# Attention scores in two halves of TensorE's array, with q and k as two fp32r parts in place of three bf16 ones

## The chip, the cores and the metric

The kernel runs on one core of one Trainium2 chip. The metric is the device time of one execution in microseconds; the span is the time from the first to the last instruction of the program in the profile. Engines are named as in the profile: PE (TensorE), DVE (VectorE), ACT (ScalarE), POOL (GpSimd), SP (SyncE, whose queue issues most DMAs).

## The reference

Four sequences of 1024 tokens with 256 features pass a linear attention block and a transformer block with a mixture of experts:

```
x = x + attn(layernorm(x))            # (x Wtheta)(x Wphi)^T (x Wg) / 16
h = rmsnorm(layernorm(x)); q, k, v = h @ wqkv     # 16 heads of 16, 4 kv heads
q, k = rope(q), rope(k)
probs = softmax(causal(q k^T / 4)); x2 = ln(x) + (probs v) @ wo
h = rmsnorm(x2); top 2 of 8 experts, weights normalised
out += (silu(h w1[e]) * (h w3[e])) @ w2[e] * weight       # FFN 512
```

The expert choice is sensitive to small errors, so scores are formed with nearly full fp32 precision.

## The kernel before

**Batches and groups.** The work is cut into four batches (one sequence each). A batch is projected (xn, gram, theta, x1, h, v, k_mm, q1_mm, q2_mm), then its four kv heads are taken one after the other as groups of four query heads (`GRP`), 16 groups in all. A group has two chunks `r` of 512 queries; a chunk has key tiles `kt` of 128 keys.

**Split and stack.** After rope (DVE), q and k are split: the sum (stage `split`, i = 0), a bf16 part (ACT), the rest (POOL), a second bf16 part (ACT), a third. In batch 0 the first and last step are on DVE, later on POOL. They go to DRAM (`qk_parts`) and come back as a stack of 96 rows: pairs of parts (`KPARTS` = 3, 2, 1, so that the products hi x hi, hi x mid, ... stand in the rows of one contraction), once for the keys and once for each of the four heads. Two more rows hold the negated row maximum. There are three stacks, for the group at work and the ones ahead.

**Maxima.** Ahead of a chunk's scores PE forms all scores in the other orientation (stage `max`, L2137 to L2145). DVE takes the maximum of each row (L1932 for the second chunk with a custom instruction that adds the mask, L1934 for the first, where PE adds the mask as a bf16 matmul of an identity). PE transposes the maxima (`maxT`), DVE negates and splits them, SP writes them into the stack.

**Scores.** For each key tile PE forms the scores of the heads (L2157, one matmul a head, one PSUM bank for up to 512 columns), ACT takes the exponential (L1440), POOL masks the diagonal tile (L1292), and PE multiplies with v (`pv`, L2171: four heads in four column tiles of the array, side by side). x1 (L2090) is the one stage that works in two 64-row tiles.

**Experts.** Routed rows are scattered to DRAM (POOL), fetched in 71 blocks of 128 rows, and a block is one round of `blockT` (L2191), `up` (L2209 to L2213), `gatedT` (L2219) and `down` (L2231 to L2237). The first blocks use fp32 weights, later ones fp32r weights in two parts. The expert's offset is read from `bexp` by PE right ahead of a block's first `up` matmul.

**Order.** A planner, `plan()`, which runs when the kernel is built, writes out one order of steps for each engine from costs (`work_of`), due times (streams with `spread_over`) and hand-set shifts of them (`NUDGE`). Each engine follows its list in order and waits on semaphores. PSUM has seven banks in a ring. Where the plan would leave PE idle it puts short filler matmuls (`warm`, L2046). The third buffer of probabilities lies over the experts' `gated` buffer, which therefore waits for batch 2.

## Time and profile before

| | |
|---|---|
| median of 3 runs | 1060.29 us (1058.63 to 1061.31) |
| the profiled execution: time | 1058.78 us |
| the profiled execution: span | 1057.1 us |
| busy: PE, DVE, ACT, POOL | 1011.6, 789.2, 661.5, 435.5 us |

A PE row of the profile has the form of the array as rows*columns: 98*128 is 98 rows of contraction and 128 columns of weights, 64*128 a matmul in one of two halves of the rows, 128*17 one of four column tiles. fp32 matmuls are profiled as two records, transposes and fp32r ones as one.

### The profile page before, as it was taken

Reading aid. Unit: us, or ns where it says so; the run is one execution under the profiler, and the core shown is the slowest. Engines: PE = TensorE matmul, PEld = TensorE weight load, DVE = VectorE, ACT = ScalarE, POOL = GpSimd, SP = SyncE. Lnnn points to the kernel's source line nnn. Section 1 sums busy time; section 2 is a strip of 40 time slices with the busy share of each in tenths; the row PEclk is TensorE's granted clock in tenths of the full one; section 3 lists DMA queues with packets and bytes.
Section 4 is the critical chain, followed back from the end, with each engine's and each line's share of the span. In section 5 each row is a group of like instructions: output and inputs, shape, how many; then the busy total and the mean of one; then the engine's idle time right before and its main releaser. Section 6 shows DMA issues by size and latency. Waiting matters only on the chain.

```text
span 1057.1 us, 19430 instructions
## 1 busy us (share of the span) xinstructions
PE 1011.6 (96%) x6264; PEld 594.6 (56%) x6264; DVE 789.2 (75%) x1701; ACT 661.5 (63%) x1305; POOL 435.5 (41%) x476
## 2 busy tenths in 40 slices
PE   5999999999999999999999999999989999999997
PEld 4765335443453333453334444456678888888886
DVE  5689979787778998899857997136776666666664
ACT  3562785747768878847767656684534555555553
POOL 1020145155732144422545325457477543444443
PEclk9999999999999999999999999999999999999999
DMA  6433114132336557732343412243434333222220
GB/s 200 128 123 103 53 46 143 55 115 77 97 109 194 146 188 212 203 95 82 111 120 109 137 25 70 52 92 82 103 78 98 73 57 52 48 47 46 48 46 11
DMA packets 86642, 102.33 MB, mean 97 GB/s; under 512 B 17904, under 2 KB 74224, under 8 KB 86544
## 3 DMA queue, kind: packets, MB, share of 16 engines
q1 hardware_dynamic: 72240, 81.46, 26.3%
q0 software_dynamic: 14304, 19.63, 10.1%
q8 instruction: 53, 0.87, 0.4%
q14 instruction: 45, 0.37, 0.1%
HBM read 56.22 MB, written 41.01 MB: 92 GB/s over the span
## 4 chain that ended last, share of the span: by engine, by line
PE 74%; DVE 16%; ACT 5%; issue 3%; DMA 1%; POOL 1%; DVEq 0%; ACTq 0%; POOLq 0%
PE psum L2171 10%; PE psum L2157 9%; PE psum L2209 6%; PE psum L2213 5%; PE psum L2137 5%; PE psum L2210 5%; DVE psum L1932 5%; PE psum L2211 5%; PE psum L2123 3%; PE psum L2219 3%; PE psum L2237 3%; PE psum L2140 2%; PE psum L2231 2%; PE psum L2233 2%; PE psum L2232 2%
## 5 line engine op out<-in xcount | busy, mean ns | idle before, releaser
L1440 ACT ACTIVATE probs_mem<-psum 128x512 f32<-128x512 f32 (+1 forms) x464 | 232.0, 584 | 90.2 <-PE psum L2157 89.0
L1932 DVE CUSTOM_DVE_ANT_1 psum<-psum,masking 128x640 f32<-128x640 f32 (+3 forms) x256 | 257.2, 1045 | 32.9 <-PE psum L2140 32.1
L1337 POOL DMA_INDIRECT out<-yout,labels x71 | 133.7, 1884 | 182.9 <-DMA out<-yout,labels 86.8
L2157 PE MATMUL psum<-stack_mem 98*128 98x512 bf16 (+3 forms) x768 | 169.3, 327 | 3.3 <-DVE mx L1932 1.8
L1292 POOL TENSOR_SCALAR_AFFINE_SELECT probs_mem<-probs_mem 128x512 f32<-128x512 f32 x104 | 66.9, 644 | 223.9 <-ACT probs_mem L1440 223.6
L2157 PEld LDWEIGHTS psum<-stack_mem 98*128 98x128 bf16 x768 | 64.6, 97 | 105.3 <-issue 21.9
L2171 PE MATMUL psum<-probs_mem,v 128*17 128x512 f32 (+3 forms) x1152 | 117.1, 490 | 0.8 <-POOL probs_mem L1292 0.5
L2015 DVE TENSOR_TENSOR w_lo<-w_mem,w_hi 128x1024 fp32r<-128x1024 f32 x51 | 62.5, 1225 | 65.5 <-PE psum L2233 57.3
L1934 DVE TENSOR_REDUCE mx<-psum 128x4 f32<-128x512 f32 (+2 forms) x96 | 96.1, 1036 | 13.1 <-PE psum L2145 10.8
L2137 PE MATMUL psum<-stack_mem 96*128 96x512 bf16 x256 | 95.2, 383 | 5.4 <-DVE mx L1932 2.6
L2209 PE MATMUL psum<-w_hi,x_hi 128*128 x216 | 93.6, 433 | 6.2 <-issue 2.4
L1440 ACT ACTIVATE gated<-psum 128x512 f32<-128x512 f32 x144 | 79.2, 612 | 24.9 <-PE psum L2157 24.9
L2210 PE MATMUL psum<-w_lo,x_hi 128*128 x216 | 85.9, 398 | 0.0
L2211 PE MATMUL psum<-w_hi,x_lo 128*128 x216 | 85.7, 397 | 0.0
L2028 DVE SCALAR_TENSOR_TENSOR gated<-gated,psum 128x512 f32<-128x512 f32 x71 | 48.3, 680 | 46.2 <-ACT gated L1465 45.9
L1458 ACT ACTIVATE yout<-psum,labels 128x256 f32<-128x256 f32 x71 | 33.8, 476 | 73.6 <-PE psum L2233 45.1
L1322 POOL DMA_INDIRECT routed<-hrow,route_mem x64 | 67.7, 1057 | 24.3 <-issue 13.4
L2140 PE MATMUL psum<-stack_mem 96*128 96x128 bf16 (+3 forms) x256 | 76.3, 298 | 0.0
L2137 PEld LDWEIGHTS psum<-stack_mem 96*128 96x128 bf16 x256 | 24.8, 97 | 76.4 <-DVE mx L1932 34.8
L2213 PE MATMUL psum<-w_mem,blockT 128*128 x136 | 65.1, 598 | 1.0 <-issue 1.0
L2231 PE MATMUL psum<-w_hi,g_hi 128*128 128x256 f32 x204 | 61.6, 302 | 0.9 <-DVE g_lo L2006 0.9
L2032 DVE TENSOR_TENSOR gated<-psum,gated 128x512 f32<-128x512 f32 x71 | 49.0, 691 | 17.9 <-PE psum L2213 11.7
(229 smaller groups left out, 2070.8 us busy)
## 6 DMA issues: line engine op xcount, KB each, us to landing
block<-routed SPq DMA_DIRECT2D x71, 129.0 KB, 2.5
w_mem<-in_w13T SPq DMA_DIRECT2D x16, 512.0 KB, 4.9
qk_parts<-w_mem SPq DMA_DIRECT2D x16, 384.0 KB, 2.9
stack_mem<-qk_parts SPq DMA_DIRECT2D x32, 192.0 KB, 3.3
w_mem<-in_x SPq DMA_DIRECT2D x8, 512.0 KB, 5.1
out<-w_mem SPq DMA_DIRECT2D x8, 512.0 KB, 4.0
x_late<-out SPq DMA_DIRECT2D x8, 512.0 KB, 5.0
stack_mem<-qk_parts SPq DMA_DIRECT2D x32, 128.0 KB, 2.7
```

What stands on the lines that cost most here:

```text
L1337: e.indirect_dma_start(out_rows, bass.IndirectOffsetOnAxis(ap=labels[w % NLABEL].bitcast(I32)[:, 0:1], axis=0), youts[w % NYOUT], None, bo ...
L1440: e.activation(probs[probs_of(m)][:, hh:hh + n, q0:CH], grid(turn[step][0][:, 0:n * (CH - q0)], n), ACT.Exp, scale=float(HD) ** -0.5).then ...
L1932: e.tensor_tensor_reduce(keys, keys, masked(w), 1.0, -3e38, ALU.add, ALU.max, to).then_inc(sem["max"], 1)
L1934: e.tensor_reduce(to, took, AX.X, ALU.max).then_inc(sem["max"], 1)
L2137: e.matmul(bk[:, 0:CH], rows_of, s[0:STACK, 0, GRP, :], start=True, stop=True)
L2140: m = e.matmul(to, rows_of, s[0:STACK, r, GRP, 0:w], start=True, stop=True)
L2157: m = e.matmul(bk[:, i * (CH - q0):(i + 1) * (CH - q0)], s[0:STACK + NMAX, kt // TPR, GRP, kt % TPR * P:(kt % TPR + 1) * P], s[0:STACK + N ...
L2171: m = e.matmul(pv_bank[32 * hh:32 * hh + HD + 1, q0:CH], v1[:, b, kt, g, :], pb[:, hh, q0:CH], start=(kt == KEYS[r][0]), stop=(kt == KEYS[ ...
L2209: e.matmul(bk, x_hi[w % 2][:, k], w13_hi[k][:, of], start=first, stop=False)
L2210: e.matmul(bk, x_hi[w % 2][:, k], w13_lo[:, k, of], start=False, stop=False)
L2211: m = e.matmul(bk, x_lo[w % 2][:, k], w13_hi[k][:, of], start=False, stop=final)
L2213: m = e.matmul(bk, blockT[w % 2][:, k], w13_s[:, k, of], start=first, stop=final)
```

## The change

- q and k are split into two fp32r parts (`KPARTS` = 2, 1): 48 rows. The rounding is by ACT, the rest is the last step; the POOL step and one ACT step of the split are gone. `qk_parts` and the stacks are fp32.
- A stack holds the keys twice, in rows 0 to 49 and in rows 64 to 113, and two heads beside each, so that heads 0 and 1 lie in the one half of the array and heads 2 and 3 in the other. `HEAD_ORDER` takes heads 0, 2, 1, 3. A load is four DMAs in place of two. fp32r matmuls are at least 256 columns wide (`formed`). Score steps cover at most two heads, where a tile of 128 columns took four.
- Two parts of a block (`youts`, `blockT`, one of `blocks`) lie over the third stack, so batch 3 has two stacks (`stack_of`), and the blocks that use them wait for batch 2's last group.
- Of norm1 and norm2 of batches 1 to 3, and of all norm3, DVE does the first steps and the seed; the Newton steps and what follows are on POOL (13 to 18 instructions in a chain). The seed is one instruction in place of two.
- PE reads the next block's offset in the middle of the second half of `up`.
- The planner has new costs for max and score (half of the columns), and new `NUDGE` values.

```diff
-KPARTS = (3, 2, 1)
+KPARTS = (2, 1)
+HALF_ROWS, NSLOTS = P // 2, GRP // 2
+HEAD_ORDER = [s + h * NSLOTS for s in range(NSLOTS) for h in range(2)]
...
-TURN, LIKE = 0.1, (3.1, 0.06)
+TURN, LIKE = 0.1, (6.9, 0.03)
...
+        columns, formed = CH + w if r else nh * w, CH + max(w, 2 * P) if r else nh * max(w, 2 * P)
+        return ("PE", formed / 4800 + 0.02 if r else formed / 4800 + nh * P / 2400 + 0.12), ...
...
-            return ("PE", n * w / 2400 + 0.01), ("ACT", 0.06 + n * w / 1200)
+            return ("PE", n * w / 4800 + 0.02), ("ACT", 0.06 + n * w / 1200)
...
 NUDGE = {
-        "aggr": {(0,): -126.5},
+        "aggr": {(3,): -18.1},
...
+                    for half in range(2):
+                        r0, heads = half * HALF_ROWS + to, slice(half * NSLOTS * CH, (half + 1) * NSLOTS * CH)
+                        e.dma_start(s[r0:r0 + nk * HD, c, NSLOTS, :], ...)
+                        e.dma_start(s[r0:r0 + nk * HD, c, 0:NSLOTS, :]..., ...)
...
+                    if r:
+                        rows = tile_rows(h0, STACK)
+                        rows_of = s[rows, r, h0 % NSLOTS, jj * P:(jj + 1) * P]
+                        e.matmul(bk[:, 0:CH], rows_of, s[rows, 0, NSLOTS, :], start=True, stop=True)
+                        m = e.matmul(bk[:, CH:CH + formed], rows_of, s[rows, r, NSLOTS, 0:formed], start=True, stop=True)
+                    else:
+                        in_bank = CH // pitch
+                        for slot_of in range(in_bank):
+                            for i in range(2):
+                                ...
+                                e.matmul(to, s[rows, r, at_slot, jj * P:(jj + 1) * P], s[rows, r, NSLOTS, 0:formed], start=slot_of == 0, stop=False)
+                        for i in range(2):
+                            own = grid(bk[:, i * CH:(i + 1) * CH], in_bank)[:, :, w - P:w]
+                            m = e.matmul(own, identb, causal.unsqueeze(1).broadcast_to([P, in_bank, P]), start=False, stop=True)
...
+                    rows, first = tile_rows(hh, STACK + NMAX), hh % NSLOTS
+                    e.matmul(grid(bk[:, 0:n * (CH - q0)], n), s[rows, kt // TPR, NSLOTS, kt % TPR * P:(kt % TPR + 1) * P],
+                             s[rows, r, first:first + n, q0:CH], start=True, stop=True).then_inc(sem["score_mm"], 1)
...
+                        if half == 1 and first and (gi, c + 1) in WORK:
+                            offset[w + 1] = e.value_load(bexp[gi][0:1, c + 1:c + 2], min_val=0, max_val=(NE - 1) * 2 * FFN)
```

How the order of instructions moves. On PE, the first chunk's maxima of a group before: L2150 is `maxT`, L2133 and L2145 the bf16 masks, L2142 and L2144 the maxima, L2171 is `pv`.

```order
L2150 MATMUL psum<-ident,mx 16x128
L2133 MATMUL psum<-masking,identb 128x512
L2142 MATMUL psum<-stack_mem 128x128 x4
L2144 MATMUL psum<-stack_mem 128x256
L2145 MATMUL psum<-masking,identb 128x128
L2144 MATMUL psum<-stack_mem 128x256
L2145 MATMUL psum<-masking,identb 128x128
```

After, at the same place (L2306 is `maxT`, L2298 the maxima in halves, L2301 the masks over the whole array, L2200 a filler):

```order
L2200 MATMUL psum<-ident 128x128
L2306 MATMUL psum<-ident,mx 16x128
L2298 MATMUL psum<-stack_mem 128x256 x4
L2301 MATMUL psum<-masking,identb 128x2x128 x2
L2298 MATMUL psum<-stack_mem 128x256 x4
L2301 MATMUL psum<-masking,identb 128x2x128 x2
L2298 MATMUL psum<-stack_mem 128x384 x2
L2301 MATMUL psum<-masking,identb 128x128 x2
```

All of the upper rows but L2150 are full-array matmuls; of the lower ones L2298 is in halves and L2301 is not, so the form changes at every row.

The second chunk's maxima among scores on PE, before (L2137 and L2140 are one unit of maxima, L2157 scores, L2171 `pv`):

```order
L2157 MATMUL psum<-stack_mem 128x128 x4
L2137 MATMUL psum<-stack_mem 128x512
L2140 MATMUL psum<-stack_mem 128x128
L2171 MATMUL psum<-gated,v 17x256 x4
L2137 MATMUL psum<-stack_mem 128x512
L2140 MATMUL psum<-stack_mem 128x128
L2157 MATMUL psum<-stack_mem 128x512 x4
```

And after (L2290 and L2291 the unit, L2313 scores, L2326 `pv`):

```order
L2313 MATMUL psum<-stack_mem 128x384
L2290 MATMUL psum<-stack_mem 128x512
L2291 MATMUL psum<-stack_mem 128x256
L2326 MATMUL psum<-gated,v 17x512 x4
L2313 MATMUL psum<-stack_mem 128x384 x3
L2290 MATMUL psum<-stack_mem 128x512
L2291 MATMUL psum<-stack_mem 128x256
L2313 MATMUL psum<-stack_mem 128x512
L2326 MATMUL psum<-probs_mem,v 17x512 x4
```

The mix is as before, but the two matmuls of a unit lie in one half, and a run in halves ends at each `pv`.

In the expert blocks on PE, before (L2219 is `gatedT`, L2209 and L2210 the first `up` matmuls):

```order
L2219 MATMUL psum<-ident,gated 128x128 x4
L2200 TENSOR_LOAD bexp
L2200 ISA x2
L2209 ISA
L2209 MATMUL psum<-w_hi_49,x_hi_58 128x512
```

And after, in the second half of a block's `up` (L2364 to L2366 are its matmuls):

```order
L2366 MATMUL psum<-w_hi_51,x_lo_61 128x512
L2370 TENSOR_LOAD bexp
L2370 ISA x2
L2364 REGISTER_ALU
L2364 MATMUL psum<-w_hi_52,x_hi_59 128x512
```

The read moved from behind the transposes to a place among the matmuls of the block before.

## Rows read from the trace of the kernel before

**Rows 1.** The page's first part: busy us, share, instructions.
```profile
PE 1011.6 (96%) x6264; PEld 594.6 (56%) x6264; DVE 789.2 (75%) x1701; ACT 661.5 (63%) x1305; POOL 435.5 (41%) x476
```
**Rows 2.** Busy time by stretch, then granted clock, DMA share, GB/s.
```profile
0.00:73.00 73.00, 60.63 (x337) 44.57 (x338) 48.76 (x192) 40.02 (x82) 12.11 (x24) 1.00 0.46 140
73.00:131.00 58.00, 56.13 (x371) 27.32 (x369) 56.71 (x129) 28.57 (x57) 5.05 (x8) 1.00 0.33 99
131.00:537.00 406.00, 392.94 (x2693) 171.17 (x2689) 343.00 (x763) 293.83 (x605) 166.47 (x194) 1.00 0.42 125
537.00:685.00 148.00, 145.14 (x931) 64.33 (x926) 99.72 (x236) 98.10 (x211) 65.76 (x81) 1.00 0.30 83
685.00:800.00 115.00, 108.66 (x487) 77.72 (x486) 68.83 (x143) 59.62 (x114) 70.54 (x65) 0.99 0.40 89
800.00:1057.00 257.00, 248.08 (x1461) 209.50 (x1459) 172.17 (x241) 141.37 (x241) 115.56 (x105) 1.00 0.30 51
```
**Rows 3.** Timeline of PE from 340 us: start, duration, then the instruction.
```profile
340.50 0.38 PE L2140 MATMUL psum<-stack_mem 96*128 96x512 bf16 x1
340.72 0.38 PE L2137 MATMUL psum<-stack_mem 96*128 96x512 bf16 x1
```
**Rows 4.** Timeline of PE from 902 us, in an expert block.
```profile
902.43 0.28 PE L2233 MATMUL psum<-w_hi,g_lo 128*128 128x256 f32 x1
902.55 0.60 PE L2219 MATMUL psum<-ident,gated 128*128 128x128 f32 x4
903.13 0.50 PE L2209 MATMUL psum<-w_hi,x_hi 128*128 x1
903.46 0.39 PE L2210 MATMUL psum<-w_lo,x_hi 128*128 x1
903.69 0.40 PE L2211 MATMUL psum<-w_hi,x_lo 128*128 x1
```
**Rows 5.** Timeline of PE from 171 us: scores, x1 in halves, a projection.
```profile
170.81 0.60 PE L2157 MATMUL psum<-stack_mem 98*128 98x512 bf16 x2
171.34 0.70 PE L2090 MATMUL psum<-w_mem 64*128 64x256 f32 x4
171.97 1.55 PE L2123 MATMUL psum<-w_mem 128*128 128x512 f32 x3
```
**Rows 6.** Timeline of the weight loads at the same place.
```profile
172.50 0.19 PEld L2123 LDWEIGHTS psum<-w_mem 128*128 128x128 f32 x1 [0.24 <-issue]
172.93 0.19 PEld L2123 LDWEIGHTS psum<-w_mem 128*128 128x128 f32 x1 [0.24 <-issue]
```
**Rows 7.** Timeline of PE from 28 us: x1's steps of batch 0.
```profile
28.04 2.19 PE L2090 MATMUL psum<-w_mem 64*128 64x256 f32 x16
30.15 0.38 PE L2046 MATMUL psum<-ident 128*128 128x128 f32 x1
```
**Rows 8.** Groups of DVE by form: busy, mean ns of one, idle before.
```profile
L1536 DVE SCALAR_TENSOR_TENSOR scales<-rt,scales 128x16 f32<-128x16 f32 x9 | 2.5, 279 | 0.3
L1536 DVE SCALAR_TENSOR_TENSOR rstd<-rt,rstd 128x8 f32<-128x8 f32 x12 | 2.0, 165 | 0.4
```
**Rows 9.** Groups of POOL by form.
```profile
L1302 POOL TENSOR_TENSOR x_late<-x_late,hrow 128x256 f32<-128x256 f32 x32 | 23.6, 757 | 29.6 <-DVE hrow L1956 29.4
L1297 POOL COPY hrow<-ids_s 128x8 int32<-128x8 int32 x3 | 1.2, 413 | 0.0
```
**Rows 10.** Groups of POOL and ACT by form: two steps of the split.
```profile
L1283 POOL TENSOR_TENSOR w_mem<-w_mem 128x512 f32<-128x512 f32 x16 | 18.4, 1163 | 15.2 <-ACT w_mem L1430 15.2
L1433 ACT ACTIVATE w_mem<-w_mem 128x512 bf16<-128x512 f32 x16 | 10.2, 638 | 2.4 <-POOL w_mem L1283 2.4
```
**Rows 11.** One line's instructions: SP's issue of a stack load, ns min/median/max.
```profile
L1141 SPq DMA_DIRECT2D stack_mem<-qk_parts x96: 429/580/1818, 62.6 to 571.7; - x96
```
**Rows 12.** Waits of the weight loads of the scores: us in total, times, longest.
```profile
PEld psum L2157 <- issue: 21.9, 48, 0.9
PEld psum L2157 <- ACT probs_mem L1440: 17.8, 44, 0.9
```

More of the change, by code:

```diff
@@ L99, with stack_of, stack_freed @@
 HEAD_GROUPS = [(b, g) for b in range(NBATCH) for g in range(NKV)]
+LAST_TRIPLE = (NBATCH - 1) * NKV
+assert LAST_TRIPLE % NSTACK == 0
+def stack_of(n):
+    if n < LAST_TRIPLE:
+        return n % NSTACK, n // NSTACK
+    return (n - LAST_TRIPLE) % 2, LAST_TRIPLE // NSTACK + (n - LAST_TRIPLE) // 2
+def stack_freed(n):
+    at, use = stack_of(n)
+    return [m for m in range(n) if stack_of(m) == (at, use - 1)]
+LAST_IN_TAIL = HEAD_GROUPS[LAST_TRIPLE - 1]
 def max_units(r):
     if r:
-        return [(jj, hh, 1, CH, (jj + 1) * P) for jj in range(TPR) for hh in range(GRP)]
+        return [(jj, hh, 1, CH, (jj + 1) * P) for jj in range(TPR) for hh in HEAD_ORDER]
     units = []
@@ L108, in max_units, with heads_of @@
         w = (jj + 1) * P
-        nh = GRP if jj < 2 else 2
-        units += [(jj, h0, nh, w if jj < 2 else CH, w) for h0 in range(0, GRP, nh)]
-    return units
+        units += [(jj, 0, GRP, CH // NSLOTS, w)] if w <= CH // NSLOTS else [(jj, s, 2, CH, w) for s in range(NSLOTS)]
+    return units
+def heads_of(unit):
+    jj, h0, nh = unit[:3]
+    return slice(h0, None if nh == 2 else h0 + nh, NSLOTS if nh == 2 else 1)
 def max_banks(r, u):
-    return 1 if not r and max_units(r)[u][0] == 0 else 2
+    return 2
 def banks_of(step):
@@ new lines @@
+        "rank": {(0,): -34.3},
+        "recip": {(1,): -57.6},
+        "recip_store": {(3,): -37.2},
+        "route": {(0,): -24.3, (1,): -32.9, (2,): 12.1},
+        "score": {(0, 0, 0): -19.1, (0, 1, 0): 0.4, (0, 2, 0): -130.5, (0, 3, 0): 13.3, (0, 3, 1): -1.8, (1, 0, 1): 3.2, (1, 1, 0): 1.5, (1, 1, 1): 0.1, (1, 2, 1):
+        -1.5, (2, 1, 1): 31.4, (2, 2, 1): -68.5, (2, 3, 0): -7.1, (3, 0, 1): -70.9, (3, 1, 0): -26.3, (3, 1, 1): -149.9, (3, 3, 0): -57},
+        "split": {(1,): -7.1},
+        "spread": {(1,): 23.1},
@@ L288 @@
+        "square": {(3,): -81.4},
+        "stack": {(0, 1, 0): -70.9, (2, 1, 0): 7.9, (2, 2, 0): 43.6, (2, 3, 0): -54.3},
+        "stats": {(3,): 31.9},
+        "stats2": {(0,): 30.2, (1,): 12.1},
+        "v": {(2,): -34.5},
+        "w2": {(): 3},
+        "weight": {(0,): 4.2},
+        "wo": {(2,): -39.1},
+        "x1": {(1,): 10.4, (2,): -5.7},
+        "xhat": {(2,): -20},
+        "xnT": {(2,): 18},
 }
@@ L538, in project @@
                 continue
-            steps += [(half, ("norm1", b, i)) for i in one_part(b, half, NORM1_STEPS)] + [(half, ("xn", b, j)) for j in (range(TPB) if b else tiles)]
+            steps += [(half, ("norm1", b, i)) for i in one_part(b, half, norm_steps("norm1", b))] + [(half, ("xn", b, j)) for j in (range(TPB) if b else tiles)]
         steps += [(2, ("gram", b, i)) for i in range(gram_steps(b))] + [(2, ("square", b, i)) for i in range(2)]
@@ L817, in over, with late @@
             return nc.alloc_sbuf_tensor_at(name, shape, F32R, offset=at)[:]
+        def late(name, n, at):
+            return nc.alloc_sbuf_tensor_at(name, [P, n], F32, offset=at)[:]
         def carve(mem, sizes):
@@ L1022, in buffer_loaded, with tile_rows @@
         def buffer_loaded(q, b, g, r):
-            n = b * NKV + g
+            at, use = stack_of(b * NKV + g)
             for c in range(r + 1):
-                q.wait_ge(f"stack{n % NSTACK}_{c}", 16 * 2 * len(KPARTS) * (n // NSTACK + 1))
+                q.wait_ge(f"stack{at}_{c}", 16 * 4 * len(KPARTS) * (use + 1))
+        def tile_rows(head, n):
+            first = head // NSLOTS * HALF_ROWS
+            return slice(first, first + n)
         def stack_read(q, b, g):
@@ L1269, in _, with norm3_rest, go_on @@
+            def norm3_rest(b):
+                q.wait_ge("norm3", NORM3_SEED * (b + 1))
+                t = rt[:, 2]
+                yield from newton("norm3_rest", rstd2, t[:, 1], t[:, 2], t[:, 3])
+            def go_on(make, b):
+                if (make, b) not in chains:
+                    chains[make, b] = make(b)
+                next(chains[make, b])
             for step in orders["POOL"]:
                 stage, *at = step
-                if stage == "split":
+                if stage == "norm1":
+                    go_on(norm1_rest, at[0])
+                elif stage == "norm2":
+                    go_on(norm2_rest, at[0])
+                elif stage == "norm3":
+                    go_on(norm3_rest, at[0])
+                elif stage == "split":
@@ L1587, in norm3 @@
                 yield
-                yield from rsqrt("norm3", rstd2, t[:, 1], t[:, 2], t[:, 3])
+                seed("norm3", rstd2, t[:, 1])
+                yield
             def route(gi):
@@ L2196, in _ @@
                     q.wait_ge("blockT_out", w + 1)
-                    if half == 0:
+                    if half == 0 and w not in offset:
                         q.wait_ge("route", routed(gi, "all"))
```

319 lines of the change are left out of this document (181 added, 138 removed), and 4 rows, old and new, of the table WORK_OF.

## The prediction

> **What bounds the kernel now.** I read the page's first two parts, then the table of stretches, then TensorE's timeline in four short windows, matmul by matmul. TensorE is busy in 96% of the span, VectorE in 75% [rows 1], at a granted clock of 1.00 in all stretches but one (0.99) [rows 2]. The table has six stretches: projection of batch 0 (to 73 us), the first maxima (to 131), attention of batches 0 to 2 (131 to 537), of batch 3 with some expert blocks (537 to 685), and expert blocks alone (685 to 1057). In 73 to 131 VectorE is the limit: 56.71 us busy of 58. In 131 to 537 both are full, TensorE 392.94 and VectorE 343.00 of 406. From 685 on VectorE has a third of its time free and TensorE has not [rows 2].
>
> "Busy" of TensorE counts a matmul's latency, so I priced it by the distance from one start to the next. A bf16 matmul of 512 columns takes 0.22 us (340.50, 340.72) [rows 3]; over many of them it is 0.216, and narrower ones are in proportion. An fp32r matmul of 512 columns takes 0.23 (903.46 to 903.69), one of 256 columns 0.12 (902.43 to 902.55); of four transposes' 0.60, some 0.16 is the last one's latency beyond its slot (as 0.28 over 0.12 in the row ahead), so they take 0.44, each 0.11 [rows 4]. Two more prices matter here. First, a change of the tile form: two bf16 matmuls and then four 64*128 ones start at 170.81 and 171.34, 0.53 us for what is 0.43 otherwise, so leaving a form costs about 0.09 [rows 5]; I use 0.092, the same between all forms here. Second, the first weights after a change are not loaded ahead: the L2123 matmul that starts at 171.97 is followed by the next load at 172.50, 0.53 later, and that by one at 172.93, 0.43 later, so 128 fp32 columns of weights cost 0.10 more once [rows 5, 6].
>
> Walking the order of TensorE's 6264 profiled matmuls with these prices gives 961 us of array time; the span is 1057. Of 131 to 537 it fills 380 of 406: 26 us are waits.
>
> **The scores and maxima.** Before, they are 294,912 columns of scores and 327,680 of maxima with their masks, 622,592 in all, by 0.216/512 us: 263 us. After, scores have as many columns, the maxima 311,296 of fp32r (narrow ones are formed 256 wide) and 32,768 of bf16 masks: 606,208 x 0.233/512 = 276 us one at a time, and 14 us of masks. The operands now have 48 or 50 rows and lie in one half of the array, so that two can run side by side. That this happens at all is in the trace: x1's 16 records of two 64-row halves take 2.11 us from 28.04 to 30.15, with 0.3 of it a wait; a pass over 512 fp32 columns takes 0.43, so one over 256 takes 0.21, and 16 in a row would need 3.4 [rows 6, 7]. But in-order issue pairs only what stands next to each other. A unit of the second chunk's maxima is two matmuls in the same half (L2290, L2291); it overlaps only with a neighbour's. Walking the changed order, matmul by matmul, 90 us of the 276 are overlapped, not 138. Term: 276 - 90 + 14 - 263 = **-63 us**.
>
> **The changes of form.** The order has 401 changes of tile form before and 735 after: score and P.V changed form already (full and column tiles), but now every bf16 mask, every transposition, projection or filler between two scores or maxima is a change too; there are 330 separate runs in halves, 96 of them of two matmuls only. 334 more changes x 0.092 = **+30 us**. Each run in halves starts with fp32r weights that nothing loaded ahead (both halves' loads go together, as x1's do): 320 such entries x 0.105 = 34, and with other fp32 entries **+39 us**. Together with five more fillers the walk gives 966 us of array time after, against 961: **+5 us**. So the doubled array gives back nearly all that it wins.
>
> The Trainium skill's "TensorEngine Tiling (Array Packing)", Overview, gives up to 2x for a contraction of 64 or less, and under Tiling Modes says that changing the mode drains TensorE. The first by itself would make the scores and maxima 152 us in place of 200, and the sum 48 lower; the second is what rows 5 price, and it speaks against this change.
>
> **The experts' offset.** Before, PE reads a block's expert right ahead of its first matmul. After the four transposes of 902.55 the next matmul comes at 903.13 where 0.44 would do, 0.14 late, and its successor 0.33 after it in place of 0.23: 0.24 us a block [rows 4]. In blocks that still use fp32 weights in one piece the read is covered. The read moves behind three matmuls of the half before, where TensorE's queue has some microseconds of work ahead: 50 blocks x 0.245 = **-12 us**. If that cover is gone, the term is 0.
>
> **VectorE and the norms.** 116 VectorE instructions go (1189 to 1073), the norm chains of batches 1 to 3 and all of norm3, at 0.17 to 0.28 us [rows 8]: 23 us off VectorE. They count only where it is the limit: 36 of them in 60 to 131, 7 us, of which I take 5 for the first maxima. In 131 to 537 about 16 us of VectorE go, under TensorE's 380: of the 26 us of waits I take 5. GpSimd gets 151 small instructions in chains of 13 to 18. No such one is in the trace: the nearest rows are a copy of 8 columns at 0.413 us and a two-operand one of 256 at 0.757 [rows 9]; from below, 0.17 as on VectorE. I take 0.35, near the first row since the width is 8 or 16: a chain takes about 6 us where VectorE's took 2.8. It stands in GpSimd's queue among masks, and ScalarE's xn, h or h2 stands behind it, and exponentials behind those. The projections are spread over a whole group's scores, so I take it as hidden; uncovered, ten chains cost up to 32 us.
>
> **The split** loses a GpSimd step of 1.163 and a ScalarE one of 0.638 [rows 10]; 24 of each are off the limit, once, before the first stack is loaded, they lie on the path. Of the 1.8 I take **-1**, since VectorE is behind at that time. ScalarE gets 32 more exponentials (four heads of 128 columns were one): 32 x 0.2 = 6 us against 15 removed, no term.
>
> **The stacks.** SP issues 64 more DMAs (659 to 723) at 0.580 us [rows 11]: 16 for a group in place of 12. Until batch 3 they are a group ahead. In batch 3 there are two stacks, so a group's load waits for the group two before: 16 x 0.58 + 3 = 12 us from there to its last maxima, while the next group's scores and expert blocks (5.8 us each) are there for TensorE. I take 0; if PE's fixed order meets a late stack, 3 to 5 us for each of two groups. The late buffers over the third stack wait for batch 2, as the blocks did for the third set of probabilities: nothing.
>
> **The sum:** +5 - 12 - 5 - 5 - 1 = -18 us. The profiled execution took 1058.78 us at a span of 1057.1; the three runs have a median of 1060.29, 1.5 above it. So 1060.3 - 18 = **1042 us**.
>
> **The rivals.**
> - *Two halves at full speed* (0.14). Waits on banks hold a score back until its neighbour is there, or the order's short runs cost less than x1's. By the page's 2x the sum is 48 lower: 994; with the weights' exposure hidden in half of the runs, 20 lower, 1022. For it: x1's loads do go in pairs. Against: every entry in rows 5 and 7 pays, and 190 of 330 runs are of two to four matmuls. I put 990 to 1022 here.
> - *No change* (0.11): the halves do what I say, and the norms on GpSimd hold ScalarE up on seven of ten chains by 2.6 us each: 1042 + 18 = 1060.
> - *Slower: the halves do not meet* (0.23). Without any overlap the order's array time is 1063, 97 more than 966, and the time 1139. A full-array matmul hid a sequencer that came 0.2 us late; a half that waits 0.2 us for its neighbour's bank runs alone. From 18 us of 90 on, one overlap in five lost, the change is slower than before; with a third lost, 1042 + 30 = 1072. For it: 21.9 us of the loads of L2157 waited for "issue" alone, and 17.8 for ScalarE [rows 12]. Against: TensorE now comes later than its plan, so banks are free when it arrives.
> - *The change does not do what it says*: a half-array matmul takes the whole array's time, that is the 1139 above (0.02 of the 0.23), since x1 shows otherwise.
> - *The forecast* (0.52): 1023 to 1057.
>
> **The range.** 0.14 lies at or below 1022, 0.23 above 1063. I leave out some 0.08 at each end: **1014 to 1082**. Around 1060.3, 0.3% is 3 us, about what such a measurement can tell: faster 0.52 + 0.14 = 0.66, same 0.11, slower 0.23.
>
> **What will show it.** In the changed trace: consecutive scores of two halves start under 0.02 us apart, the next pair 0.23 later; the first pair of a run takes 0.33; about 735 changes of form; time of scores and maxima near 200 us plus 70 for changes. The block in the last stretch takes 4.87 us, not 5.12. VectorE is busy about 766 us. If the first group's end (131 us) is not 5 us earlier, the VectorE term is wrong; if 131 to 537 grows, overlap is lost; if ScalarE waits for GpSimd in xn or h, the chains are not hidden. The forecast is wrong if the waits of 131 to 537 do not stay near 25 us.

## The result and the profile after

The changed kernel took 1106.7, 1109.7, 1128.3 and 1128.3 us, median 1119.0, against 1059.6 for the kernel before on the same chip. The ratio is 1.046, 95% interval 1.042 to 1.049, made without the two executions of 1128, in which the granted clock was 0.93 in place of 0.95. Its fastest execution is 47 us slower than the kernel before; 1042 was forecast and 1082 was the upper end of the range.

The profiled execution (1109.7 us, span 1108.0) has, in the page's first two parts, PE's busy share and, over 40 slices of the span, the clock that TensorE was granted in tenths:

```profile
PE 1055.0 (95%) x6130; PEld 636.1 (57%) x6130; DVE 773.0 (70%) x1585; ACT 654.7 (59%) x1313; POOL 429.7 (39%) x603
```

```profile
PEclk9998999799999989896889999799999999999999
```

PE is as busy as before [rows 1]. But the clock row has dips to 6, 7 and 8. By stretch (busy us of each engine, then clock, DMA share, GB/s; groups 1 to 11 now end at 581, batch 3 at 757):

```profile
73.00:131.00 58.00, 56.46 (x316) 29.79 (x314) 48.74 (x108) 27.27 (x58) 16.71 (x32) 0.94 0.40 118
131.00:581.00 450.00, 433.17 (x2632) 206.84 (x2632) 331.72 (x703) 289.21 (x608) 158.74 (x246) 0.92 0.41 120
581.00:756.00 175.00, 169.47 (x948) 76.71 (x946) 109.17 (x238) 103.67 (x224) 72.81 (x100) 0.94 0.29 77
756.00:1057.00 301.00, 294.52 (x1660) 243.18 (x1660) 207.31 (x328) 172.84 (x308) 150.45 (x160) 0.99 0.35 71
```

Before, the clock was 1.00 or 0.99 in every stretch [rows 2]. Now it is 0.92 to 0.94 wherever scores and maxima run, and 0.99 among the expert blocks. A mean of 0.92 is two levels mixed. This shows in narrow windows, cut where the clock changes:

```profile
196.00:209.50 13.50, 12.27 (x71) 6.03 (x72) 11.10 (x24) 8.29 (x17) 4.05 (x4) 1.00 0.11 33
209.50:223.10 13.60, 13.60 (x48) 6.19 (x46) 3.35 (x6) 3.35 (x7) 0.19 (x1) 0.50 0.00 0
223.10:236.00 12.90, 12.90 (x79) 6.98 (x78) 9.27 (x17) 5.86 (x14) 6.94 (x6) 1.00 0.18 42
492.90:506.50 13.60, 12.42 (x90) 5.18 (x82) 11.49 (x28) 8.49 (x20) 1.27 (x2) 1.00 0.30 90
506.50:533.70 27.20, 27.02 (x117) 10.96 (x116) 16.25 (x60) 15.26 (x34) 3.82 (x6) 0.50 0.25 70
```

The clock is at 1.00 (2.4 GHz) or at 0.50 (1.2 GHz). In the stretch at 0.50 PE counts as busy for all 13.60 us and gets through 48 matmuls, where it got through 71 just ahead. The mix of matmuls is not the same in the two rows, so here is one group of eight records of `pv`, first in a stretch at 0.50 and then in one at 1.00:

```profile
506.86 1.91 PE L2326 MATMUL psum<-probs_mem,v 128*17 128x512 f32 x8 [0.16 <-ACT probs_mem L1587]
419.96 1.05 PE L2326 MATMUL psum<-probs_mem,v 128*17 128x512 f32 x8
```

The same work takes nearly twice as long, and VectorE and ScalarE, busy for 3.35 us each of the 13.60, stand behind PE. There are eleven such stretches, of which the last lies in the span's last 4 us; the ten others have 99 us together. At half clock PE does half the work, so they cost up to 49.5 us, which is the whole distance between the two kernels. Before there was one of 3.4 us, among the expert blocks (and one in the span's last microsecond).

What PE did ahead of a fall, in its timeline (start, duration, the instruction, idle time before it):

```profile
503.33 0.72 PE L2298 MATMUL psum<-stack_mem 48*128 48x512 f32 x2
503.98 0.29 PE L2301 MATMUL psum<-masking,identb 128*128 128x128 bf16 x2
504.50 0.50 PE L2313 MATMUL psum<-stack_mem 50*128 50x512 f32 x2 [0.23 <-ACT probs_mem L1587]
504.94 0.20 PE L2340 MATMUL psum<-route_mem,before 128*128 128x64 bf16 x1
504.97 0.19 PE L2341 MATMUL psum<-route_mem,onesb 128*128 128x64 bf16 x1
505.68 1.02 PE L2313 MATMUL psum<-stack_mem 50*128 50x512 f32 x4 [0.51 <-ACT probs_mem L1587]
```

Scores and maxima in halves, with waits of 0.2 to 0.5 us for ScalarE's banks. Waits of that size stood before too [rows 12], and the clock stayed at 1.00.

### The profile page after: what moved, and what is told of

It reads as the page before. It is cut to its first block, busy times and chain, and to the rows that moved or that the text cites. A ratio compares the mean times of both kernels' runs of the same rounds, so it can differ in the third digit from the quotient of the medians.

```text
span 1108.0 us, 19213 instructions
## 1 busy us (share of the span) xinstructions
PE 1055.0 (95%) x6130; PEld 636.1 (57%) x6130; DVE 773.0 (70%) x1585; ACT 654.7 (59%) x1313; POOL 429.7 (39%) x603
## 4 chain that ended last, share of the span: by engine, by line
PE 86%; DVE 4%; ACT 4%; issue 2%; DMA 2%; POOL 1%; DVEq 0%; ACTq 0%; POOLq 0%
PE psum L2326 14%; PE psum L2313 11%; PE psum L2290 6%; PE psum L2364 4%; PE psum L2366 4%; PE psum L2365 4%; PE psum L2277 4%; PE psum L2368 4%; PE psum L2298 3%; PE psum L2333 3%; PE psum L2214 3%; PE psum L2291 3%; PE psum L2376 2%; ACT probs_mem L1587 2%; PE psum L2388 2%
## 5 line engine op out<-in xcount | busy, mean ns | idle before, releaser
L1587 ACT ACTIVATE probs_mem<-psum 128x512 f32<-128x512 f32 (+2 forms) x496 | 236.7, 554 | 122.4 <-PE psum L2313 115.2
L2313 PE MATMUL psum<-stack_mem 50*128 50x512 f32 (+2 forms) x640 | 192.6, 461 | 15.2 <-ACT probs_mem L1587 9.5
L1488 POOL DMA_INDIRECT out<-yout,labels x71 | 118.1, 1663 | 176.5 <-DMA out<-yout,labels 115.7
L2313 PEld LDWEIGHTS psum<-stack_mem 50*128 50x128 f32 x640 | 91.1, 199 | 99.8 <-ACT probs_mem L1587 41.3
L2326 PE MATMUL psum<-probs_mem,v 128*17 128x512 f32 (+3 forms) x1152 | 130.2, 533 | 1.8 <-POOL probs_mem L1443 1.3
L2290 PE MATMUL psum<-stack_mem 48*128 48x512 f32 x256 | 106.2, 509 | 3.1 <-DVE mx L2086 2.4
L2088 DVE TENSOR_REDUCE mx<-psum 128x4 f32<-128x512 f32 (+2 forms) x96 | 96.5, 1042 | 18.0 <-PE psum L2301 17.2
L2364 PE MATMUL psum<-w_hi,x_hi 128*128 x216 | 91.6, 424 | 3.3 <-DVE x_lo L2156 2.9
L2290 PEld LDWEIGHTS psum<-stack_mem 48*128 48x128 f32 x256 | 42.8, 196 | 79.5 <-issue 27.6
L2366 PE MATMUL psum<-w_hi,x_lo 128*128 x216 | 85.3, 395 | 0.0
L2182 DVE SCALAR_TENSOR_TENSOR gated<-gated,psum 128x512 f32<-128x512 f32 x71 | 48.3, 680 | 42.4 <-ACT gated L1612 37.2
L1473 POOL DMA_INDIRECT routed<-hrow,route_mem x64 | 64.7, 1012 | 27.3 <-issue 15.2
L2291 PE MATMUL psum<-stack_mem 48*128 48x256 f32 (+2 forms) x256 | 73.4, 341 | 0.0
L2368 PE MATMUL psum<-w_mem,blockT 128*128 x136 | 69.4, 631 | 1.6 <-DVE gated L2182 0.9
```

The costliest lines, as they stand in the source:

```text
L1488: e.indirect_dma_start(out_rows, bass.IndirectOffsetOnAxis(ap=labels[w % NLABEL].bitcast(I32)[:, 0:1], axis=0), youts[w % NYOUT], None, bo ...
L1587: e.activation(probs[probs_of(m)][:, hh:hh + n, q0:CH], grid(turn[step][0][:, 0:n * (CH - q0)], n), ACT.Exp, scale=float(HD) ** -0.5).then ...
L2088: e.tensor_reduce(to, took, AX.X, ALU.max).then_inc(sem["max"], 1)
L2290: e.matmul(bk[:, 0:CH], rows_of, s[rows, 0, NSLOTS, :], start=True, stop=True)
L2291: m = e.matmul(bk[:, CH:CH + formed], rows_of, s[rows, r, NSLOTS, 0:formed], start=True, stop=True)
L2313: e.matmul(grid(bk[:, 0:n * (CH - q0)], n), s[rows, kt // TPR, NSLOTS, kt % TPR * P:(kt % TPR + 1) * P], s[rows, r, first:first + n, q0:CH ...
```

## The experiments

**1. The early read alone.** In the kernel before:

```diff
-                    if half == 0:
+                    if half == 0 and w not in offset:
...
+                        if half == 1 and first and (gi, c + 1) in WORK:
+                            offset[w + 1] = e.value_load(bexp[gi][0:1, c + 1:c + 2], min_val=0, max_val=(NE - 1) * 2 * FFN)
```

> The kernel before, with one part of the change alone: PE reads the next block's expert in the second half of up. If that read was on the path in the blocks with split weights (0.245 us in each of 50), the block period falls from 5.12 to 4.87 us and the time by 12 us, to 1048 (1045 to 1051). If the time lay beside other work, or if other parts of the change are what made the blocks shorter, the period stays at 5.12 and the time at 1060.

Measured: 1044.0 us (1041.4 to 1046.0) against 1059.4, ratio 0.985 (0.983 to 0.987). The median block period of the last stretch is 4.87 us where it was 5.12. The time is a little below the range expected. The changed kernel has the same 4.87, and its timeline shows why: behind the four transposes the next matmul starts 0.36 us later, where it took 0.58 [rows 4].

```profile
879.37 0.28 PE L2390 MATMUL psum<-w_hi,g_lo 128*128 128x256 f32 x1
879.49 0.60 PE L2376 MATMUL psum<-ident,gated 128*128 128x128 f32 x4
879.85 0.48 PE L2364 MATMUL psum<-w_hi,x_hi 128*128 x1
```

So this part is right, and the rest of the change costs some 65 us. This kernel is the fastest of all here and beats both.

**2. Heads in the order 0, 1, 2, 3.**

```diff
-HEAD_ORDER = [s + h * NSLOTS for s in range(NSLOTS) for h in range(2)]
+HEAD_ORDER = list(range(GRP))
...
-                        for slot_of in range(in_bank):
-                            for i in range(2):
+                        for i in range(2):
+                            for slot_of in range(in_bank):
```

> The changed kernel with heads taken in the order 0, 1, 2, 3, so that two matmuls of one half stand side by side more often: the order of the steps is the same on every engine, and the walk of PE's order gives 985 us of array time in place of 966. Theory A (a half leaves the other half of the array idle, and where PE also waits, the clock falls for want of work in the array): the clock stays at 0.95 or falls further, and the time rises by 5 to 20 us, to 1113 to 1130. Theory B (it is PE's waits alone that bring the clock down, whatever the form of the array): the longer matmuls fill the waits, so the clock rises to 0.97 or more and the time does not rise, 1085 to 1108. Theory C (the clock has nothing to do with the order): it may show any level, also in the kernel before of the same chip.

Measured: 1133.6 us (1130.0 to 1140.5), ratio 1.070 (1.067 to 1.075), clock 0.933. It has 150 us at half clock ahead of its end, the changed kernel 99: up to 25 us, about the whole rise. Theory B's rise of the clock did not come. A has the sign, and its upper end of 1130 is passed by 4 us.

**3. The norm chains back on DVE, in one piece behind the seed.**

```diff
                     seed("norm1", s[:, 0], s[:, 1])
+                    if b:
+                        for _ in norm1_rest(b):
+                            pass
                     yield
```

> The changed kernel, with the rest of each norm chain on DVE right behind its seed, in the same places of the order; GpSimd does none of it. If the prediction's step holds (the chains on GpSimd are hidden and DVE's relief is worth little), the time is within 5 us of the changed kernel, or up to 10 us above it because DVE now does 137 more instructions. If the chains on GpSimd hold up ScalarE (the profile shows 6.8 us of such waits), it is up to 7 us faster. The granted clock does not hang on this: 0.95 in both.

Measured: 1167.8 us (1151.2 to 1175.3), ratio 1.093 (1.086 to 1.101), clock 0.922. Both expectations missed by far, in time and in clock: the ratios are 1.093 and 1.046, some 50 us apart. The profiled execution is 41.5 us longer than that of the changed kernel, and it has 174 us at half clock ahead of its end where that had 99: up to 37 of the 41 us can be the clock. So a delay on another engine comes back as lost clock.

**4. Forms of the array by themselves.** PE alone, 512 columns a matmul, twelve rounds of each form, waits as described:

```
full   98 rows, bf16, 8 a round          pairs  50 rows, fp32r, 16 a round, halves in turn
wide   128 rows, fp32r, 8 a round        lone   50 rows, fp32r, 8 a round, one half only
```

> No part of the reference is computed: PE alone runs stretches of matmuls of 512 columns, each after 96 full-array ones that bring the clock to 1.00. Forms: full (98 rows, bf16), wide (128 rows, fp32r), pairs (50 rows, fp32r, in alternate halves), lone (50 rows, fp32r, one half only), and rounds of four scores and four pv matmuls, full or in pairs. Each comes without waits, with a short wait a round and with a longer one (ScalarE copies 512 columns and PE waits for it), at the same stream time a round. Theory A: lone falls to half clock where full and wide of the same waits stay at 1.00; pairs stay up longer than lone. Theory B: all forms fall together, at the same wait. Prices: a pair of halves every 0.23 us, a lone half every 0.23 us.

Windows, in this order: full, wide, pairs and lone without waits; wide, pairs and lone with the longer wait in each round (twelve rounds of each); last, ten rounds without waits that go between pairs and `pv` matmuls, a change of form every 0.8 us:

```profile
28.20:49.00 20.80, 20.80 (x98) 9.44 (x97) 0.00 (x0) 0.00 (x0) 0.00 (x0) 1.00 0.00 0
69.50:91.50 22.00, 22.00 (x99) 18.05 (x98) 0.00 (x0) 0.00 (x0) 0.00 (x0) 1.00 0.00 1
112.30:134.30 22.00, 22.00 (x194) 19.11 (x194) 0.00 (x0) 0.00 (x0) 0.00 (x0) 1.00 0.00 1
155.10:192.30 37.20, 37.20 (x97) 28.61 (x96) 0.00 (x0) 0.00 (x0) 0.00 (x0) 0.56 0.00 0
477.80:510.90 33.10, 25.20 (x99) 17.15 (x98) 0.00 (x0) 6.92 (x11) 0.00 (x0) 1.00 0.00 0
531.70:565.00 33.30, 25.35 (x194) 17.09 (x193) 0.00 (x0) 6.92 (x11) 0.00 (x0) 1.00 0.00 1
585.80:636.40 50.60, 42.70 (x98) 27.75 (x98) 0.00 (x0) 6.92 (x11) 0.00 (x0) 0.54 0.00 0
719.30:752.20 32.90, 32.90 (x242) 8.59 (x241) 0.00 (x0) 0.00 (x0) 0.00 (x0) 1.00 0.00 0
```

In the fourth row PE is never idle: matmul follows matmul in one half, and the clock falls all the same, soon after the first of them, and stays down. In the fifth row PE stands still for a quarter of the time, in the whole array's form, and keeps 1.00. Pairs keep it too, and 192 of them take the 22.0 us that 96 wide ones take: two halves do run at the time of one. Changes of form without waits keep it too (last row). Theory A holds, B is out as the only cause.

**5. The two orders without any wait.** The matmuls of groups 1 to 11 in before's order and in the changed one, by PE alone.

> No part of the reference is computed: PE alone runs the matmuls of groups 1 to 11, form by form, first in the order of the kernel before and then in that of the changed one, with no waits on other engines, each behind 96 full-array matmuls. The walk of the orders gives 379.6 us of array time for the first and 376.7 for the second. If the walk's prices hold, both take that within 3 us. Clock: if a half alone is enough to lose it in these orders, the second falls below 1.00 here too; if it takes halves together with PE's waits, both stay at 1.00.

```profile
29.40:408.20 378.80, 378.80 (x2690) 175.56 (x2688) 0.00 (x0) 0.00 (x0) 0.00 (x0) 1.00 0.00 1
428.90:796.60 367.70, 367.70 (x2612) 180.59 (x2611) 0.00 (x0) 0.00 (x0) 0.00 (x0) 1.00 0.00 1
```

Before's order takes what the walk said, the changed one 9 us less. It has 484 changes of form where before's has 266, and many lone halves, and without waits neither costs it the clock.

**6. All rows of the array, the same order.** In the changed kernel:

```diff
-                        rows = tile_rows(h0, STACK)
+                        rows = slice(0, P)
...
-                    rows, first = tile_rows(hh, STACK + NMAX), hh % NSLOTS
+                    rows, first = slice(0, P), hh % NSLOTS
```

The stacks are filled with zeros first, so that the added rows add nothing, and the rope tables are zeros, as in run 7.

> The changed kernel with the same order of steps on every engine, but scores and maxima over all 128 rows of the array (two heads in one contraction), and with rope tables of zeros, so that all scores are zero: scores, probabilities and the experts' rows are not the reference's. The walk gives 1081 us of array time, 115 more than the changed kernel's, since nothing runs side by side. Theory A (a half leaves array work out, and that loses the clock): the granted clock goes back to 0.99 or 1.00, and the time is 1081 and some 55 to 75 us of waits, 1135 to 1155. Theory B (PE's waits at the other engines' banks lose it): those waits remain in part, and the clock stays at 0.97 or below.

Measured: 1088.9 us (1088.5, 1089.4), ratio 1.029 (1.026 to 1.032), clock 1.00. The expectation's 1081 for the walk was an error of mine (transposes and fillers had the price of full matmuls); with the prices of the prediction it is 1006, 40 more than the changed kernel's 966. So by the walk PE has 40 us more to do, waits on the same engines in the same order, and the kernel is 18 us faster than the fastest execution of the changed one (11 us faster than the faster one of run 7, which has the same values). Theory A is right on the clock; its time, 1135 or more, was at least 46 us too high. Its stretch of groups 1 to 11:

```profile
131.00:581.00 450.00, 440.22 (x2709) 248.41 (x2708) 341.12 (x715) 295.69 (x618) 162.95 (x253) 1.00 0.42 121
```

**7. Control: only the scores set to zero.** Rope tables of zeros in the changed kernel.

> The changed kernel with rope tables of zeros alone (all scores zero, the rest as in the run on full forms): a control. If neither the clock nor the time hangs on the values, it is as the changed kernel, 1107 to 1128 us at 0.93 to 0.955.

Measured: 1099.8 and 1128.9 us, the second at a clock of 0.932. The clock falls with all scores zero too, so the values are not its cause. 1099.8 lies 7 us below the range expected: from two executions, a small effect of the values, or of chance, is not told apart.

**8. Halves in the kernel before.**

```diff
-                        rows_of = s[0:STACK, r, h0 + c, jj * P:(jj + 1) * P]
+                        rows_of = s[0:48, r, h0 + c, jj * P:(jj + 1) * P]
```

and in the same way the other operands of maxima and scores.

> The kernel before, with the bf16 scores and maxima over rows 0 to 49 alone (one half of the array, part of the products left out) and zero rope tables, so that its values are not the reference's. Order, streams and waits are as before; 517 more changes of form add 57 us to the walk (1018 in place of 961). Theory A: the granted clock falls below 0.95 and the time is 1150 or more. Theory B: the clock stays at 0.99 or 1.00, since PE waits no more than before, and the time is 1100 to 1120.

Measured: 1208.5 us (1205.1, 1212.0), ratio 1.142, clock 0.892. In the stretch of rows 2's 131 to 537:

```profile
131.00:537.00 406.00, 399.93 (x2044) 145.49 (x2040) 266.38 (x564) 233.13 (x465) 129.65 (x144) 0.80 0.32 95
```

As theory A had it. The order and the columns are before's; one half of the array is left out, and a clock of 1.00 becomes 0.80. The 517 more changes of form came with it (918 in place of 401), so this run alone does not say which of the two it was.

**9. Paired maxima.** Where the banks allow it, PE issues two units of opposite halves together (100 of 128 times):

```diff
+                    for k in range(2):
+                        for to, stationary, moving in (first[k], second[k]):
+                            m = e.matmul(to, stationary, moving, start=True, stop=True)
```

> The changed kernel with one change on PE: where the banks allow it (100 of 128 times), two units of the second chunk's maxima that lie in opposite halves are issued together, so that their four matmuls run as two pairs and not as four lone halves. The rest is as in the changed kernel, and the values too. The walk of PE's order gives 941 us of array time in place of 966. Theory A (lone halves with PE's waits lose the clock): the granted clock rises to 0.97 or more and the time falls by 25 us and by part of the 50 that the clock costs, to 1045 to 1080. Theory B (waits alone): shorter streams leave longer waits, so the clock stays at 0.95 or falls, and the time is 1095 to 1115.

Measured: 1188.0 us (1174.6 to 1197.9), ratio 1.112 (1.109 to 1.115), clock 0.893 in the profiled execution. A miss on both sides, though theory B had the sign of the clock: array time went down and the time up by some 70 us over the changed kernel (ratios 1.112 and 1.046). In the changed kernel the maxima's loads waited 25.4 us for VectorE; here (L2227 is that load):

```profile
PEld psum L2227 <- DVE mx L2086: 44.5, 38, 2.2
```

Two units need four banks at once, and PE waits longer in one piece: 44.5 us in 38 waits is 1.2 us each, where 25.4 in 37 was 0.7. There are 252 us at half clock ahead of the end, where there were 99.

**10. The norms on DVE, at full clock.** Run 6 with the edit of run 3.

> As the run on full forms (scores and maxima over all rows of the array, all scores zero, values not the reference's), which keeps its clock at 1.00, but with the rest of each norm chain on DVE right behind its seed, as in the run on the norms. If the 60 us that the move back to DVE cost there came mostly through the clock, it costs 12 us or less here: 1085 to 1101 at a clock of 1.00. If the norms on DVE cost that much by themselves, the time is 1130 or more. If the prediction's step was right in size, it is 1089 to 1094.

Measured: 1114.4 us (1109.3 to 1118.1), ratio 1.052 (1.050 to 1.055), 25 us above run 6, between the expectations. But the clock was not full here: 0.995 in the profiled execution, 0.986 to 0.992 in the other three. The profiled one is 20 us above run 6's and has 10 us at half clock ahead of its end, so about 15 us of its loss are not the clock's. In run 3 it was some 50: the clock made most of that loss and not all of it.

**11. The two orders with the same waits.**

> No part of the reference is computed: the replay of groups 1 to 11 by PE alone, before's order and the changed one, but with a wait of PE for a copy by ScalarE (0.8 us) after every 36 matmuls, and then both again with one after every 18. If halves and waits together lose the clock, the changed order falls below 1.00 with the waits, and before's order stays at 1.00 with the same ones (or falls far less). If waits alone do it, both fall alike. At full clock the stretches take 379 and 368 us and 0.8 us for each wait: some 420 and 410 with the first, 460 and 450 with the second.

Windows: before's order and the changed one with 55 and 52 waits, then with 110 and 105 (the count of ScalarE's copies):

```profile
29.40:466.70 437.30, 397.41 (x2690) 175.90 (x2689) 0.00 (x0) 34.60 (x55) 0.00 (x0) 1.00 0.00 1
487.70:948.60 460.90, 423.28 (x2611) 195.88 (x2610) 0.00 (x0) 32.72 (x52) 0.00 (x0) 0.90 0.00 1
969.50:1465.00 495.50, 415.74 (x2690) 175.62 (x2689) 0.00 (x0) 69.20 (x110) 0.00 (x0) 1.00 0.00 1
1486.00:2043.40 557.40, 481.37 (x2611) 214.08 (x2610) 0.00 (x0) 66.06 (x105) 0.00 (x0) 0.84 0.00 1
```

Without waits the changed order is 11 us shorter (run 5). With the first waits it is 24 longer, with the second 62, at 0.90 and 0.84, where before's order with the same waits keeps 1.00. So the changed order together with waits loses the clock, where neither does it alone. What in that order does it is not settled: it differs from before's in its halves and also in its changes of form, and no run here has as many changes, with waits, and no halves.

**12. The norms on GpSimd in the kernel before, planned as in the change**, with the early read.

```diff
+        return (("POOL", 0.2),) if at[1] >= seed and (at[0] or stage == "norm3") else (("DVE", 0.08),)
```

> The kernel before with two parts of the change and no halves: the early read of the expert, and the norm chains on GpSimd behind a seed of one instruction, planned as in the change (the planner moves some steps for it). The run with the early read alone took 1044.0. If the norms are worth what the prediction took (5 us at the first maxima, 5 in the attention), 1034 to 1042. If they are worth what the two moves back to DVE suggest (25 us in the run on full forms), 1020 to 1030. If the planner's other order, for which the hand-set shifts of before were not made, costs more than they bring, 1045 to 1060. The clock stays at 0.99 or 1.00 in all three.

Measured: 1060.6 us (1059.4 to 1064.0), ratio 1.001 (1.000 to 1.002), clock 0.995, nearest to the third case expected. The gain of the early read (15 us) is gone.

**13. The same chains with every engine's order kept.** Each chain goes in one piece into GpSimd's queue where its seed stands:

```diff
+                while rests and (step == ("end",) or rests[0][0] < at_step[step]):
+                    _, name, b = rests.pop(0)
+                    for _ in {"norm1": norm1_rest, "norm2": norm2_rest, "norm3": norm3_rest}[name](b):
+                        pass
```

> The kernel before with the early read, every engine's order kept as it was, and the rest of each norm chain (batches 1 to 3, and all of the third norm) taken off DVE and put in one piece into GpSimd's queue, at the place where its seed stands in the plan. With the early read alone it was 1044.0; with the norms and a new plan 1060.6. If that loss of 16 us came from the planner's other order, this one is 1034 to 1044. If it is the chains on GpSimd, which is slower in each step and holds masks and the splits behind them, this one is 1050 to 1062.

Measured: 1059.1 us (1056.2 to 1060.5), ratio 0.999 (0.998 to 1.000), clock 0.988. It is the chains and their place in GpSimd's queue, not the new plan. GpSimd's timeline of run 1 and then of this run, around the first chain:

```profile
61.73 1.15 POOL L1283 TENSOR_TENSOR w_mem<-w_mem 64x512 f32<-64x512 f32 x1 [5.20 <-ACT w_mem L1430]
69.19 1.16 POOL L1283 TENSOR_TENSOR w_mem<-w_mem 128x512 f32<-128x512 f32 x1 [6.32 <-ACT w_mem L1430]
```

```profile
65.67 0.20 POOL L1324 TENSOR_TENSOR rt<-rt 128x8 f32<-128x8 f32 x1
65.83 1.15 POOL L1384 TENSOR_TENSOR w_mem<-w_mem 64x512 f32<-64x512 f32 x1
73.08 1.16 POOL L1384 TENSOR_TENSOR w_mem<-w_mem 128x512 f32<-128x512 f32 x1 [6.10 <-ACT w_mem L1531]
```

L1283 and L1384 are the same split step. It stands behind the chain and comes 4.1 us later, the next one 3.9; the first group ends 5.6 us later, at 137.0 in place of 131.4. What lies between is in PE's timeline, of run 1 and then of this run:

```profile
66.53 1.10 PE L2068 MATMUL psum<-w_mem 128*128 128x256 f32 x4 [0.68 <-ACT w_mem L1401]
69.53 2.05 PE L2186 MATMUL psum<-w_mem 128*128 128x256 f32 x4 [3.90 <-ACT w_mem L1502]
```

ScalarE waits for the late split, PE waits for ScalarE, 3.90 us in one piece where it was 0.68, and in that wait the clock falls to 0.50, from 68.2 to 75.0:

```profile
68.20:75.00 6.80, 5.47 (x12) 1.94 (x12) 3.75 (x7) 4.52 (x10) 1.16 (x1) 0.50 0.29 68
```

The same happens in a wait of 3.71 us that begins at 242.4. In all this run has 24 us at half clock ahead of its end, run 1 has 3.4. So up to 10 of the 15 us lost are the clock's, in a kernel whose scores and maxima use full forms.

**14. Paired and changed order with the same waits.**

> No part of the reference is computed: PE alone replays groups 1 to 11 in the order of the changed kernel and in that of the one with paired maxima, first without waits, then with a wait for ScalarE's copy after every 36 matmuls, then after every 18. The walk gives 376.8 us for the first order and 358.6 for the second. If a lone half is what loses the clock, the paired order keeps more of it than the changed one at the same waits: above 0.90 with the first and above 0.84 with the second, and it takes 18 us or more less. If what counts is the work in the array over the time, pairing leaves the work as it is and shortens the time it is spread over, so that it keeps at least as much clock here, and the loss in the kernel with paired maxima came from PE waiting longer there (44.5 us for VectorE in place of 18.9): then too it is the faster one here. Only if pairs themselves lose the clock does the paired order fall below the changed one.

Windows: changed and paired order, first without waits, then with 105 each:

```profile
30.20:397.60 367.40, 367.40 (x2611) 180.38 (x2610) 0.00 (x0) 0.00 (x0) 0.00 (x0) 1.00 0.00 1
418.60:779.40 360.80, 360.80 (x2609) 175.98 (x2608) 0.00 (x0) 0.00 (x0) 0.00 (x0) 1.00 0.00 1
...
1735.00:2304.00 569.00, 492.94 (x2611) 218.87 (x2608) 0.00 (x0) 66.06 (x105) 0.00 (x0) 0.81 0.00 1
2325.00:2870.30 545.30, 469.18 (x2608) 205.03 (x2606) 0.00 (x0) 66.06 (x105) 0.00 (x0) 0.84 0.00 1
```

Pairs do not lose the clock by themselves: at the same waits the paired order has 0.84 to 0.81, and with 52 waits 0.93 to 0.93; it takes 24 and 8 us less. They hardly save it either, so that lone maxima are at most a small part of what loses it, as far as one execution can tell. The changes of form are nearly as many (476 and 484), which leaves them, and the other halves, as candidates. So the loss of run 9 came with its longer waits, as far as this replay can tell. The changed order's 0.81 here and 0.84 in run 11 show how far the same program varies.

## Why the prediction was wrong

**The step that failed.** The prediction priced every matmul of the changed kernel at the rate of the rows before, "at a granted clock of 1.00 in all stretches but one", and had no term for the clock. Halving the time in the array was taken as a gain of 63 us. But with scores and maxima in halves and PE also waiting for banks, the clock falls (runs 6, 8 and 11): 99 us at half clock, up to 49.5 us, and in the best case 1060 without it. No rival had this. The one on the slow side (0.23) said that the halves would not meet; they do (runs 4 and 5), and its sign was right for a wrong reason. The answer was not to be had from before's trace alone, since nothing there runs long in halves: x1's 2.11 us [rows 7] kept their clock. A rule could have raised the question: the Trainium skill ("TensorE: Matmul & The Clock Gate", Part 1: The HAM clock gate) says that a hardware monitor sets the clock by how busy the engine has been. The profile's busy share is not that measure: it is 95% here, and 100% in run 4's fourth row.

**The array walk.** It held. Groups 1 to 11 without waits take 378.8 and 367.7 us against a walk of 379.6 and 376.7; the second is 9 us less than walked, from more overlap or cheaper changes of form, which the runs do not tell apart. The Trainium skill's "TensorEngine Tiling (Array Packing)", Overview, gives up to 2x, and run 4's pairs show it (192 in 22.0 us). The drain that the Trainium skill's same page, Tiling Modes, gives for a change of mode is in the walk as the changes of form: 735, as forecast.

**The waits of 131 to 537.** "25 us" was wrong. Group by group, distance less walk less half of the time at half clock gives 43 us for groups 1 to 15, by the same sum 32 before. With the replays of run 5 in place of the walk, groups 1 to 11 alone have some 45 us of waits, and had 27. Over the attention the weight loads' waits for ScalarE grew from 60 to 97 us, and those for VectorE fell from 65 to 38: the scores' loads waited for its exponentials 17.8 us before [rows 12] and 41.3 after (in part at half clock). Shorter matmuls meet the same exponentials earlier, as the rival on banks had it, at a smaller size; this reading was not tried by itself.

**The experts' offset.** Right in mechanism and period, 4.87 as forecast. The term was -12; alone it brought 15.4 (run 1). By the groups' ends, 684.6 in run 1 and 684.2 before, all of it lies behind the attention.

**VectorE and the norms.** Forecast as -10 in two parts, with the chains hidden on GpSimd. The first group ends at 134.1, 3 us later than before, not 5 earlier (3.4 of it are the clock's), and 773.0 us busy are near the 766 forecast. VectorE has the 116 instructions fewer (the profile counts 1701 and 1585, not the prediction's 1189 and 1073). A step on GpSimd takes 0.20 to 0.26 us, 0.29 from start to start, not 0.35, but "hidden" was wrong where a split stands behind it: moved alone, the chains cost 15 us, of which up to 10 through the clock (runs 12 and 13). Moved back in one piece in the kernel of run 6, they cost 25, at a clock a little below full (run 10). Each order is made for one place of the chains, and both moves disturb it. What the norms' move is worth by itself, in an order tuned for it, stays open.

**The split and the stacks.** -1 and 0 were not tried by themselves. None of PE's waits in the profile after is put down to a DMA, so no late stack is seen.

**The sum**, for the profiled execution and from the same walk: clock +48 over before's, waits of groups 1 to 15 +11, array time +4 or 5, last stretch beyond its array time and the clock -13, first group without the clock -1 or 2: 49 of the 51 us between the spans 1057.1 and 1108.0. So without the clock the change is worth some 0 to +3 us and not the -18 forecast: the offset came as forecast, and the waits of TensorE, taken at -10 for VectorE's relief, came out some 10 higher than before. The clock is the larger of the two errors.

## What to carry to other kernels

Work in halves of the array can be worth its factor where PE does not wait, or where pairs follow each other evenly (run 4). In a mixed order, where other engines set the pace, waits that were free in full forms can halve the clock, and then each of them costs again. Full forms are not safe from it either, as the two falls in single waits of 3.90 and 3.71 us show (run 13). So look at the granted clock of the stretch, not at the busy share, and first time the order in the new form without waits and with some put in (runs 5 and 11): one short kernel would have given the sign. And what is moved to a less busy engine has to be priced by what stands behind it in that engine's queue.

## What the runs showed of the hardware

- A stretch of matmuls in one half of the array, back to back and with PE 100% busy, loses the clock: 96 of them take 37.2 us where 96 full-row ones take 22.0 (run 4).
- A kernel with 40 us more work for PE (by the walk) in full rows was 18 us faster than the one in halves, 11 us than the same with its scores set to zero (runs 6 and 7).
- The same program varies once its clock falls: 1106.7 to 1128.3 us for the changed kernel, 1174.6 to 1197.9 for run 9, while the kernel before stayed within 1057.7 and 1063.1 in all its runs here.
- Delays grow: a move that costs 25 us at a clock of 0.986 to 0.995 cost some 50 where the clock was 0.92 or less (runs 10 and 3).
- With scores and maxima in full forms too, the clock fell to half in waits of 3.90 and 3.71 us in one piece, and the kernel had 24 us at half clock (run 13).
